# Eight sequences through two transformer layers on one core: second and third FFN layers from fp32 to three fp32r products of split operands

## What is computed

```python
def _L0_ffn_ref(x, w1_w, w1_s, w2_w, w2_s, h1_w, h1_s, h2_w, h2_s, w3_w, w3_s):
    def _tlin(x, w, s):
        return jnp.einsum('bsi,oi->bso', x, w) * s
    h = jax.nn.silu(_tlin(x, w1_w, w1_s)) * _tlin(x, w2_w, w2_s)
    h = jax.nn.gelu(_tlin(h, h1_w, h1_s), approximate=False)
    h = jax.nn.gelu(_tlin(h, h2_w, h2_s), approximate=False)
    return _tlin(h, w3_w, w3_s)
```

## Time and profile before

| | |
|---|---|
| median of 3 runs | 1327.5 us (1322.08 to 1331.36) |
| the profiled execution, its own time | 1324.73 us |
| span of the profile | 1323.0 us |
| TensorE clock granted, mean | 0.986 |
| busy: PE, DVE, ACT, POOL | 93%, 61%, 54%, 44% |
| from one sequence's dense stage to the next | 136.1 us (398.9 to 535.0 us of the span) |

### The profile page before, as it was taken

One profiled execution on the slowest core, in us unless ns is written; L12 is line 12 of the kernel. 1 busy time (PEld: TensorE's weight loads), 2 busy tenths in 40 slices (PEclk: granted clock), 3 DMA queues, 4 the chain that ended last, 5 costly groups with the idle time before them and its releaser, 6 DMA issues.

```text
span 1323.0 us, 26477 instructions
## 1 busy us (share of the span) xinstructions
PE 1236.3 (93%) x9090; PEld 868.2 (66%) x9090; DVE 811.9 (61%) x3384; ACT 717.0 (54%) x1535; POOL 587.4 (44%) x776
## 2 busy tenths in 40 slices
PE   5988999999999999999999999999999967899997
PEld 2565576657765776567656765666566657886896
DVE  4064487638853885388637863686458756775563
ACT  2366167725772577247734774367437624457675
POOL 7133154415442544254425442444235334675577
PEclk9999999999999999999999999999999988999999
DMA  7603320233023402340234014400530045542233
GB/s 223 165 3 105 111 69 7 91 103 97 9 89 88 112 11 81 96 110 13 82 96 108 14 62 116 106 16 26 152 103 19 3 145 125 81 72 36 38 55 41
DMA packets 84085, 101.84 MB, mean 77 GB/s; under 512 B 12537, under 2 KB 45217, under 8 KB 83873
## 3 DMA queue, kind: packets, MB, share of 16 engines
q1 hardware_dynamic: 65360, 82.22, 23.0%
q0 software_dynamic: 13792, 9.54, 5.0%
q10 hardware_dynamic: 4800, 8.39, 1.9%
HBM read 55.44 MB, written 46.37 MB: 77 GB/s over the span
## 4 chain that ended last, share of the span: by engine, by line
PE 73%; ACT 7%; DVE 6%; issue 5%; DMA 5%; POOL 3%; SPq 1%; DVEq 0%; POOLq 0%; ACTq 0%
PE bank L646 22%; PE bank L639 16%; PE heads L703 13%; PE bank L628 7%; ACT probs L1044 4%; PE bank L624 4%; PE bank L979 3%; PE bank L987 3%; PE bank L633 1%; DMA Q<-slots_of_q 1%; DMA W_s<-in_W 1%; POOL out L1277 1%; PE bank L753 1%; PE bank L745 1%; DVE probs L1471 1%
## 5 line engine op out<-in xcount | busy, mean ns | idle before, releaser
L1044 ACT ACTIVATE probs<-bank 128x512 f32<-128x512 f32 (+2 forms) x896 | 441.8, 581 | 218.0 <-PE bank L646 212.2
L1224 POOL TENSOR_SCALAR_AFFINE_SELECT probs<-probs 128x384 f32<-128x384 f32 x256 | 127.4, 520 | 270.4 <-ACT probs L1044 269.4
L646 PE MATMUL bank<-K,Q 128*128 128x192 f32 (+4 forms) x1024 | 240.1, 312 | 1.7 <-issue 1.7
L646 PE MATMUL bank<-Q,K 128*128 128x192 f32 (+4 forms) x1024 | 219.3, 320 | 2.1 <-issue 1.6
L703 PE MATMUL heads<-probs,V 128*9 128x192 f32 (+4 forms) x3072 | 195.6, 396 | 9.3 <-DVE probs L1471 5.1
L646 PEld LDWEIGHTS bank<-K,Q 128*128 128x128 f32 x1024 | 166.4, 189 | 26.8 <-issue 15.4
L646 PEld LDWEIGHTS bank<-Q,K 128*128 128x128 f32 x1024 | 151.4, 193 | 36.3 <-issue 21.5
L1034 ACT ACTIVATE probs<-bank,sh_s 128x512 f32<-128x512 f32 x64 | 44.0, 687 | 210.1 <-PE bank L639 199.4
L703 PEld LDWEIGHTS heads<-probs,V 128*9 128x9 f32 x3072 | 76.1, 91 | 119.2 <-issue 79.7
L1277 POOL DMA_INDIRECT out<-h1T_s x78 | 123.3, 1581 | 58.2 <-ACT h1T_s L1185 33.8
L646 PE MATMUL bank<-QM,K 128*128 128x512 f32 (+3 forms) x512 | 138.0, 333 | 11.2 <-DVE mx_s L1419 5.3
(11 more groups left out here) (202 smaller groups left out, 2025.0 us busy)
## 6 DMA issues: line engine op xcount, KB each, us to landing
Q<-slots_of_q SPq DMA_DIRECT2D x15, 1024.0 KB, 10.4
K<-slots_of_k SPq DMA_DIRECT2D x60, 192.0 KB
QM<-slots_of_qm SPq DMA_DIRECT2D x8, 1024.0 KB, 8.7
slots_of_q<-Q SPq DMA_DIRECT2D x24, 256.0 KB, 3.0
slots_of_k<-QM SPq DMA_DIRECT2D x24, 256.0 KB, 3.9
slots_of_qm<-Q SPq DMA_DIRECT2D x24, 256.0 KB, 4.1
slots_of_k<-Q SPq DMA_DIRECT2D x24, 256.0 KB
slots_of_q<-Q ACTq DMA_DIRECT2D x24, 256.0 KB
```

The costliest lines, as they stand in the source:

```text
L646: mm = pe.matmul(to[:, at:at + right.shape[1]], left, right, start=True, stop=True, skip_group_check=True)
L1044: return act.activation(to, bank, func, scale=scale, bias=bias).then_inc(taken_sem(run, unit), 1)
L1224: pool.affine_select(out=three, in_=three, compare_op=ALU.is_ge, fill=0.0, base=0, pattern=[[0, 3], [1, P]], channel_multiplier=-1)
```

## The change

The second and third FFN layers of the sequences 1 to 7 go from one fp32 matmul per block to three fp32r matmuls: weights and inputs are each split into a high part (rounded to fp32r) and a low part (the rest), and high x high, low weight x high input and high weight x low input are summed in the bank. `dense` (4 fp32 matmuls of 512 columns a unit) becomes `dense_low` (12 fp32r ones). Sequence 0 keeps `dense`.

- Weights: POOL splits h1T and h2T once (`split_weights`). The low parts are saved to DRAM and loaded again by SP for each sequence (`load_low`, 1 MB each) into one half of K1 and of K2 while that half holds no keys.
- Inputs of the second layer: DVE writes the gated values whole into K1's lower half, ACT rounds them (`a_high`, four operations), DVE makes the low part in place (`low_gate`, four). Inputs of the third: ACT takes each h1 bank twice with Gelu, once whole and once rounded, and DVE makes the low part (`low_hidden`, four).
- The keys' zeros and ones under the low parts are made anew: POOL sets K1's lower half to zero after h1_3 and K2's upper half after h2_3 (4096 elements a partition each), and `fetch` brings the rows back in two halves, the restored one with 32 rows in place of 24. PE waits for both halves of K1 ahead of the pairs, and for K2's upper half at cmax 20.
- The first FFN layer moves from slide unit 14 to 15 (`GATES_AT`).

The core of the diff:

```diff
-            def fetch(name, groups=slice(0, G), sem="slots"):
+            def fetch(name, groups=slice(0, G), sem="slots", restored=False):
...
+                    by_row, rows = scratch[name].rearrange("(g i) r t -> i r g t", i=HG), 4 * D if restored else 3 * D
...
                 if this and after:
+                    sp.wait_ge(taken_sem(run, SLIDE_UNITS[GATES_AT]), taken_at(run, SLIDE_UNITS[GATES_AT]))
+                    load_low("h1", low_h1)
+                    if before:
+                        sp.wait_ge(taken_sem(run, CAUSAL_UNITS[-1]), taken_at(run, CAUSAL_UNITS[-1]))
+                        load_low("h2", low_h2)
                     load_x((b, 1), (b + 2) & (NB - 1))
...
-                    fetch_sent((b, 1), "k1")
+                    sp.wait_ge(S["sent_k1"], due("sent_k1", (b, 1), SENT))
+                    fetch("k1", UPPER, "upper")
                     fetch_sent((b, 1), "qm1")
                     fetch_sent((b, 1), "q1")
+                    if this:
+                        sp.wait_ge(S["keys1_restored"], due("keys1_restored", (b, 0), 1))
+                    fetch("k1", LOWER, restored=True)
...
-                        fetch_sent((b, 0), "k2")
+                        sp.wait_ge(S["sent_k2"], due("sent_k2", (b, 0), SENT))
+                        fetch("k2", LOWER)
                         fetch_sent((b, 0), "q2")
+                        sp.wait_ge(S["keys2_restored"], due("keys2_restored", (b, 0), 1))
+                        fetch("k2", UPPER, "upper", restored=True)
...
+            def dense_low(run, unit, layer, c, terms=range(3 * FC)):
+                w, w_low, x, x_low = layer
+                to = bank_of(run, unit) if terms[0] else to_bank(run, unit)
+                for n in terms:
+                    left, right = ((w, x), (w_low, x), (w, x_low))[n // FC]
+                    mm = pe.matmul(to[:, :], left[:, n % FC, c * P:(c + 1) * P], right[n % FC], start=(n == 0), stop=(n == 3 * FC - 1))
...
-                    dense(run, "h2_0", h2T, hidden_b, 0)
+                    dense_low(run, "h2_0", layer2, 0, range(2 * FC))
+                    pe.wait_ge(S["b_low"], due("b_low", now, FC))
+                    dense_low(run, "h2_0", layer2, 0, range(2 * FC, 3 * FC))
...
+                    if GATES_AT + 3 <= n < GATES_AT + 3 + FC and this and after:
+                        c = n - GATES_AT - 3
+                        act.wait_ge(taken_sem(run, f"up{c}"), taken_at(run, f"up{c}"))
+                        act.activation(high_a[c], whole_a[:, c, :], ACT.Identity).then_inc(S["a_high"], 1)
...
                     for c in range(FC):
-                        gelu(run, f"h1_{c}", hidden_b[c], sh1[:, c:c + 1])
+                        if this:
+                            evacuate(run, f"h1_{c}", whole_b[:, c, :], ACT.Gelu, scale=sh1[:, c:c + 1])
+                        gelu(run, f"h1_{c}", high_b[c] if this else hidden_b[c], sh1[:, c:c + 1])
...
+            def split_weights(nth, w, to, high, low, last):
+                opening = ("opening", -1)
+                pool.wait_ge(full_sem(opening, last), full_at(opening, last))
+                pool.tensor_copy(high, w[:, :, :]).then_inc(S["split_laps"], 1)
+                pool.wait_ge(S["split_laps"], 2 * nth - 1)
+                pool.tensor_tensor(low, w[:, :, :], high.bitcast(F32), ALU.subtract).then_inc(S["low_made"], 1)
+                pool.wait_ge(S["low_made"], nth)
+                pool.tensor_copy(to[:, :, :], high.bitcast(F32)).then_inc(S["whole_split"], 1)
...
+                if after:
+                    pool.wait_ge(full_sem(run, "h1_3"), full_at(run, "h1_3"))
+                    pool.memset(K1[:, HALVES["k1"], :].bitcast(F32), 0.0).then_inc(S["keys1_restored"], 1)
                 power(now, 2)
...
+                if after:
+                    pool.wait_ge(full_sem(run, "h2_3"), full_at(run, "h2_3"))
+                    pool.memset(K2b[:, HALVES["k2"], :].bitcast(F32), 0.0).then_inc(S["keys2_restored"], 1)
                 pool.wait_ge(S["shifted"], due("shifted", now, 1))
                 pool.tensor_tensor(ex[:, :, :], euler[:, :, :], lgs[:, :, :], ALU.pow).then_inc(S["exped"], 1)
                 fill_rows(now)
...
+                    if GATES_AT + 5 <= n < GATES_AT + 5 + FC and this and after:
+                        low_gate(now, n - GATES_AT - 5)
```

More of the change, by code:

```diff
@@ L150, in slide_order @@
         units += [f"cols{CAUSAL}"] if n == 13 and before else []
-        units += [f"{which}{c}" for c in range(FC) for which in ("gate", "up")] if n == 14 and after else []
+        units += [f"{which}{c}" for c in range(FC) for which in ("gate", "up")] if n == GATES_AT and after else []
         units += ["mixed_causal"] if n == 18 and before else []
@@ L896, in dense_stage @@
                         wait_taken(run, f"h1_{c}")
-                    if not this:
-                        pe.wait_ge(S["h2_weights"], 16 * HIDDEN_LOADS)
-                    dense(run, "h2_0", h2T, hidden_b, 0)
-                if this:
-                    mix_first(run)
-                if this and not after:
+                    if part != "first":
+                        pe.wait_ge(S["low_h2"], due("low_h2", (b, -1), 16))
+                    dense_low(run, "h2_0", layer2, 0, range(2 * FC))
@@ L903, in dense_stage @@
+                    pe.wait_ge(S["b_low"], due("b_low", now, FC))
+                    dense_low(run, "h2_0", layer2, 0, range(2 * FC, 3 * FC))
+                mix_first(run)
+                if after:
+                    dense_low(run, "h2_1", layer2, 1)
+                    dense_low(run, "h2_2", layer2, 2, range(6))
+                else:
                     begin_tiles(run)
                     run_tiles(0, MIXED)
+                pe.wait_ge(S["hrow2"], due("hrow2", now, 1))
+                turn(run, "hT2", lambda t: hrow[:, t, :])
@@ L928, in dense_stage @@
+                    dense_low(run, "h2_2", layer2, 2, range(9, 3 * FC))
+                else:
+                    run_tiles(MIXED, QUERIED)
+                pe.wait_ge(S["xn2"], due("xn2", now, 1))
+                turn(run, "xnT2", lambda t: xn[:, t, :])
+                project_rows(run, "v2", hT, wv1[:, :])
+                wait_taken(run, "xnT2")
+                project_rows(run, "logits", xnT, wgT[:, :], E)
                 if after:
-                    dense(run, "h2_3", h2T, hidden_b, 3)
+                    dense_low(run, "h2_3", layer2, 3)
+                else:
+                    run_tiles(QUERIED, ROUTED)
@@ L1122, in slide_stage @@
                         split_hi(run, nxt, "qm1")
[L1123 removed]
+                    if n == GATES_AT and after:
                         if not this:
@@ L1718, in dense_stage @@
                 now, nxt = (b, 0), (b, 1)
+                low = this and after
                 if this:
                     divide_rows(run, now, SLIDE, 2)
+                    if low:
+                        low_hidden(run, now, 0)
                     copy_heads(now, SLIDE, 3)
```

179 lines of the change are left out of this document (112 added, 67 removed).

## The result

The changed kernel takes 1361.46 us (median of 4 runs, 1357.45 to 1366.82), the kernel before 1325.6 in the same measurement: ratio 1.027, 95% interval 1.022 to 1.032, slower by some 36 us. The forecast was 1350, slower, with 1316 to 1372 as its range. The profiled execution took 1360.81 us, with a span of 1359.1. What the prediction named is there, close to its size; some 9 us more come once, in sequence 0, where it had counted nothing.

What follows compares the result with a forecast made beforehand. PE, busy 93% of the span, was taken to bound the kernel, with DVE to watch where pairs begin. Per sequence -3.31 + 0.8 + 4.27 + 1.5 = +3.26 us, seven times +22.8 on 1327.5: 1350 us, range 1316 to 1372.

Steps and rivals of the forecast that it cites:

- The unit of twelve: Dense stage: twelve fp32r matmuls at 0.225 us take 2.70 us, saving 0.73 against an fp32 unit's 3.43.
- the upper bound: Dense stage: an fp32r matmul costs 0.253 us, as in the score burst; as a rival 1365 us, chance 0.12.
- h2_0 and hrow: Dense stage: second Gelu adds 0.69 us to PE's 0.54 wait ahead of h2_0; hrow leaves about 0.35 of 1.10 saved.
- The slide stage: ACT's four copies and DVE's four subtractions cost 0 to 2.4 us, taken 0.8: one subtraction ahead of the heads' mask.
- POOL's second memset: After h2_3: clearing half of K2, 3.50 us, delays exponentials, place_rows and DVE's release of PE's bank: +4.27 us a sequence.
- The clock: Behind PE's wait of about 6 us, PE may run at half speed some 4 us: 0 to 2.5, taken 1.5.
- The sum: A sequence: -3.31 + 0.8 + 4.27 + 1.5 = +3.26 us, seven times +22.8.
- the rival that gives the stall back: Pairs stage: idle DVE and PE time works off the backlog; 3.5 us given back makes 1315 us; chance 0.16.
- the rival with little won and little lost: Clock stays up and the slide stage hides all: -3.31 + 4.27 = +1 us a sequence, 1334 us; chance 0.15.
- the low weights: Rival at h1_0: the 1 MB loads land late, 2 us if loads and sends came in a row, 1364 us; chance 0.04.
- the sum with all costs high: Whole kernel, costs high and savings low: -1.6 + 1.5 + 4.6 + 2.5 = +7 us a sequence, 1376 us.
- The step that failed: Opening and sequence 0: POOL's weight splitting runs while POOL is idle, a delay of 0 to 3 us once, taken as 0.

Runs made afterwards that it cites:

- experiment 7: Experiment 6 with ACT's rounded Gelu ahead of the whole one and h2_0 waiting for the rounded ones only: 1304.31 us (0.984).
- experiment 9: Against experiment 5, only the Gelu order changed, rounded first, without moving the subtractions: 1303.97 us (0.982).
- experiment 6: Against experiment 5, DVE's four gated-value subtractions moved behind the heads' mask, PE waiting for them only ahead of h1_0's last four matmuls: 1308.37 us (0.987).
- Experiment 1: Changed kernel with POOL's memset of K2's upper half moved behind the exponentials and the experts' rows: 1341.77 us (1.011).
- Experiment 3: Changed kernel with fourteen idle fp32r matmuls a sequence on PE, where the long wait behind third_layer was: 1360.37 us (1.025).
- experiment 2: Changed kernel with h2T's splitting and the clearing of K2's lower half in six pieces between sequence 0's masks: 1350.8 us (1.018).
- Experiment 8: Against experiment 4, DVE's 8-element cast of slot_i made a two-input tensor_tensor, same place beside the memset: 1319.67 us (0.995).
- experiment 4: Changed kernel with the edits of experiment 1 and experiment 2 together: 1333.33 us (1.004).
- experiment 5: Against experiment 4, POOL's memset of K2's upper half moved behind the next pairs stage's second mask and row, where DVE reads PSUM only: 1309.33 us (0.988).

## Why the prediction was right, and where it was short

- *The unit of twelve.* Predicted 2.70, measured 2.81 to 2.85: 0.234 a matmul, between the taken 0.225 and the upper bound 0.253. Up to h2_3 2.8 us were saved, 3.31 predicted: the five units that carry the saving (h1 and h2_0) are each 0.11 to 0.15 us longer than taken, which is enough for the difference. The Trainium skill, "TensorE: Matmul & The Clock Gate", section "Wait — 56ns, not 53.3ns?", has 215.7 ns; the runs give 234 for fp32r, and the measurement decides.
- *h2_0 and hrow.* 1.2 us predicted, 1.23 measured; the wait for hrow appeared. Experiments 7 and 9 confirm that the second Gelu stood there: without it ahead of h2_0 the wait is 0.34.
- *The slide stage.* +0.8 predicted, +0.9 measured (1.59 in place of 0.66 us). The reason, one subtraction ahead of the mask, was only half of it: experiment 6 moved them and DVE was late elsewhere.
- *POOL's second memset.* From h2_3 to the score unit behind both waits it was to be 17.73 us, +4.27; it is 17.43 (586.98 to 604.41), +3.97. The predicted 6 us of waits in two pieces are 3.45 + 1.26. Experiment 1 shows that the order on POOL made it.
- *The clock.* 1.5 us taken. From the score unit to the next sequence's gates it is 1.8 us longer (72.2 and not 70.4), and there lie 5.6 us at half clock. Experiment 3 separates it: 138.4 us a period with the clock up, 139.9 with it down, so 1.5.
- *The sum.* 3.26 us a sequence predicted, 3.65 measured over six periods; the rival that gives the stall back fell, and so did the rival with little won and little lost; the low weights never show as a wait. No large error hides another: the saving was taken 0.5 too high and the stall 0.3 too high, which partly cancel and leave most of the 0.4 between 3.26 and 3.65. One bound was added up wrongly: the sum with all costs high takes 1.5 us for the slide stage, where its own term goes up to 2.4, so it should end near 1383 and not 1376, and the stated 1372 lies below both. The middle does not hang on it.
- *The step that failed*: "POOL's splitting of the weights runs in the opening and in sequence 0, where POOL is idle; a delay of 0 to 3 us once, taken as 0." It looked at the engine that does the work and not at its neighbour. Measured: 8.6 us, 10.7 by experiment 2. With it the forecast would have been 1359. The Trainium skill, "SBUF — State Buffer", section "Who interferes with whom", states it: VectorE and GpSimd share a pair of ports; a copy, cast or tensor_scalar of VectorE from SBUF to SBUF can take both, and then the one that comes second is blocked, while an operation with two inputs in SBUF meets only GpSimd's reads. Experiment 8 agrees on the form. On who comes second the records don't bear it out: in experiment 1 the cast's record begins 0.03 us ahead of the memset's (586.45 and 586.48), and it is the cast that waits.
- From the seventh dense stage to the end 5.6 us were added. 3.6 of them come up to the first experts' tokens of the tail (145.5 and 149.1 us), as in any other period, and 2.0 in the tail behind it (233.5 and 235.5), where the mean granted clock was 0.95 before and 0.93 now. Why it was lower there is open; in experiment 3 the same tail took 233.0.

## What to carry to other kernels

A faster product in the dense stage was worth 1.2% once its helpers stood in the right place, and cost 2.7% when they did not: price every added operation by what is queued behind it on its engine, then by the engine beside it. Before GpSimd's idle time is used, look at what VectorE does in it: in these runs DVE's reads of PSUM beside a memset lost nothing (0.69 us), a cast and tensor_scalars within SBUF did, and a 0.17 us operation became a 3.57 us one. Changing the form of that small operation cost nothing: it takes 0.17 us as a tensor_tensor too.

## What the runs showed of the hardware that was not expected

- A cast of 8 elements on DVE waits out a memset on POOL (3.57 us against 3.51), a tensor_tensor in its place does not (0.17). The four tensor_scalars of 9.52 us stood through three POOL instructions in a row: they begin within the subtraction and end behind the memset. Read one by one, the first ends at 100.74 with the subtraction, and the other three not before 106.14, behind the cast and the memset: between those two DVE did not get in.
- Where DVE reads two inputs in SBUF and POOL masks in SBUF, they take turns. DVE and POOL of the changed kernel in the slide stage:

```profile
549.52 0.68 DVE L1739 TENSOR_TENSOR K<-W_s,probs_high 128x512 fp32r<-128x512 f32 x1
...
550.72 1.13 DVE L1739 TENSOR_TENSOR K<-W_s,probs_high 128x512 fp32r<-128x512 f32 x1
```

```profile
550.42 0.90 POOL L1320 TENSOR_SCALAR_AFFINE_SELECT probs<-probs 128x512 f32<-128x512 f32 x1 [0.91 <-ACT probs L1118]
551.27 1.09 POOL L1322 TENSOR_SCALAR_AFFINE_SELECT probs<-probs 128x512 f32<-128x512 f32 x1
```

  DVE's first row has nothing of POOL beside it, and a mask of POOL alone takes 0.66 us (537.49). The other rows overlap, and their ends follow each other by turns: POOL at 551.32, DVE at 551.85, POOL at 552.36, about 0.5 us apart. Each record holds the other engine's turn and then its own. The kernel before has it too, where POOL shows 1.10 us for such a mask; the change adds rows of DVE that meet it:

```profile
533.87 1.10 POOL L1238 TENSOR_SCALAR_AFFINE_SELECT probs<-probs 128x512 f32<-128x512 f32 x1
```

- The clock. Two waits of 1.28 to 1.56 and 0.61 to 1.26 us with 1.6 us of work between them brought it to its lower level in every sequence of experiments 1 and 4. One wait of 1.00 us never did so in experiment 5, nor did the one of 1.26 in experiment 8 that is shown. One of 1.53 did in some sequences and not in others (0.83 and 1.00 in the windows of experiment 8), so a single wait of that length is not safe.
